# A transformer layer on one core: attention steps in one fixed form, with maxima on row tiles, projections at step ends, and row scaling on ScalarE

## What is computed

```
x = x + layernorm(attention(layernorm(x)))
x = x + layernorm(ffn(layernorm(x)))

attention: kqv = x @ Wqkv + bqkv            (16 heads of 32)
  scores = k . q / sqrt(32), kept where t >= s, else -10000
  attn = softmax(scores, axis=2); out = attn^T v; out @ Wo + bo
ffn: h = silu(x @ Wg^T) * (x @ Wu^T), h @ Wd^T
  with weights (int - 128) * scale, 2048 hidden
```

## Time and profile before

| | |
|---|---|
| median of 3 runs | 1860.55 us |
| the profiled execution | 1863.75 us |
| its span, first to last instruction | 1862.0 us |
| mean granted TensorE clock | 0.971 |
| busy: PE, DVE, ACT, POOL | 1719.7, 1062.0, 716.1, 332.4 us |
| chain that ended last, by engine | PE 72%, DVE 16%, ACT 3%, issue 3%, DMA 2% |
| first score of group 0 | at 114.92 us |
| first matmul of the feed-forward part | at 1156.63 us |

### The profile page before, as it was taken

How to read it: one execution, slowest core, us unless ns; L and a number is a source line. 1 busy time by engine, 2 the same in 40 slices (tenths; PEclk the granted TensorE clock), 3 DMA queues, 4 the chain that set the end, 5 groups by cost and what they waited for, 6 DMA issues and landing times.

```text
span 1862.0 us, 25259 instructions
## 1 busy us (share of the span) xinstructions
PE 1719.7 (92%) x10015; PEld 782.5 (42%) x10016; DVE 1062.0 (57%) x1779; ACT 716.1 (38%) x1271; POOL 332.4 (18%) x558
## 2 busy tenths in 40 slices
PE   3889899998899989899989788999999999999997
PEld 1433333343333333233333223555555555555554
DVE  5545864685864686765695576724343333434254
ACT  3335555444555445555435454222222222222221
POOL 2212222133222223222222133100000000000000
PEclk7989999999999999899999989999999999999999
DMA  5111111122111222101222255311010100101000
GB/s 175 35 35 36 37 44 35 47 74 86 51 31 35 59 70 78 51 19 35 69 68 69 58 189 161 120 35 45 23 46 29 40 35 34 40 30 39 29 23 23
DMA packets 59174, 104.17 MB, mean 56 GB/s; under 512 B 11440, under 2 KB 11440, under 8 KB 59056
## 3 DMA queue, kind: packets, MB, share of 16 engines
q1 hardware_dynamic: 59056, 102.56, 18.3%
HBM read 51.92 MB, written 25.17 MB: 41 GB/s over the span
## 4 chain that ended last, share of the span: by engine, by line
PE 72%; DVE 16%; ACT 3%; issue 3%; DMA 2%; SPq 2%; POOL 1%; DVEq 0%; ACTq 0%; POOLq 0%
PE ps L669 24%; PE ps L686 13%; PE ps L578 8%; PE ps L634 6%; PE ps L644 6%; DVE mcol L872 5%; PE ps L601 4%; PE ps L620 4%; PE ps L589 4%; DVE st L779 2%; PE ps L655 2%; SPq L469 2%; DVE rec L900 2%; ACT pt L748 1%; PE ps L559 1%
## 5 line engine op out<-in xcount | busy, mean ns | idle before, releaser
L748 ACT ACTIVATE pt<-ps,nrm 128x512 f32<-128x512 f32 (+3 forms) x768 | 389.5, 584 | 363.7 <-PE ps L620 363.4
L669 PE MATMUL ps<-x2in,gu 128*128 128x512 f16 x2048 | 463.9, 380 | 0.0
L872 DVE TENSOR_REDUCE mcol<-ps 128x1 f32<-128x512 f32 (+3 forms) x608 | 357.4, 650 | 141.0 <-PE ps L604 128.4
L669 PEld LDWEIGHTS ps<-x2in,gu 128*128 128x128 f16 x2048 | 190.8, 98 | 244.4 <-issue 31.6
L601 PE MATMUL ps<-kpack,qpack 96*128 96x512 f16 (+3 forms) x768 | 218.3, 333 | 47.9 <-DVE yt L910 17.9
L944 DVE SCALAR_TENSOR_TENSOR hf<-ps,usc,sg 128x512 f32<-128x512 f32 x128 | 96.2, 751 | 270.0 <-PE ps L669 268.7
L686 PE MATMUL ps<-wd,hh 128*128 128x512 f32 x512 | 224.0, 438 | 0.0
L620 PE MATMUL ps<-qpack,kpack 98*128 98x512 f16 (+3 forms) x768 | 201.3, 335 | 18.5 <-DMA qpack<-mt 8.2
L686 PE MATMUL ps<-wd,hl 128*128 128x512 f32 x512 | 200.7, 392 | 0.0
L994 POOL TENSOR_SCALAR rs<-mv 128x1 f32<-128x1 f32 x128 | 26.3, 205 | 921.5 <-DVE mv L781 921.5
L634 PE MATMUL ps<-pt,v 128*32 128x512 f32 (+3 forms) x1536 | 172.4, 522 | 17.4 <-DVE atf L896 14.8
(11 more groups left out here) (103 smaller groups left out, 1622.8 us busy)
## 6 DMA issues: line engine op xcount, KB each, us to landing
qpack<-stage SPq DMA_DIRECT2D x192, 64.0 KB, 2.0
kpack<-stage SPq DMA_DIRECT2D x192, 64.0 KB, 2.0
xin<-in_x SPq DMA_DIRECT2D x32, 256.0 KB, 2.6
xr<-in_x SPq DMA_DIRECT2D x32, 256.0 KB, 2.9
x1d<-x SPq DMA_DIRECT2D x32, 256.0 KB, 3.2
x2d<-x2s SPq DMA_DIRECT2D x32, 256.0 KB, 2.0
x2in<-x2d SPq DMA_DIRECT2D x8, 1024.0 KB, 5.6
x1in<-x1d SPq DMA_DIRECT2D x8, 1024.0 KB, 5.7
```

The source lines that it names most:

```text
L669: mm = pe.matmul(bk, GU[:, c, m, i * 128:(i + 1) * 128], x2in[:, 1 - k, :, p, c, :], start=p == 0 and c == 0, stop=p == 1 and c == 3)
L748: act.activation(Pt[:, (step - 1) % 2, h, off:512], ps[:, BANK[job], off:512], ACT.Exp, scale=esc).then_inc(s_ex, 1)
L872: dve.tensor_reduce(mcol[:, n % 2, col:col + step * (nh - 1) + 1:step], ps[:, BANK[job], 0:nh * w].rearrange("p (h k) -> p h k", h=nh), AX ...
```

## The change

- **Steps of one form.** Each step is now: one lot of maxima, den and num of the step before, four scores, what closes a half, row work, at most one projection at its end. Den and num thus stand ahead of the scores of the step, where they stood behind them. `projections` puts one projection at the end of the steps of width 512 and 384 (with gaps where there are fewer), none at the narrow ones. woproj are spread over the last group of their sequence and the first two of the next; `atT` has a fifth slot for that.
- **Row-tiled maxima.** A lot is now one block of queries for four heads: four matmuls with K = 32 on four row tiles (`tile_position`), each into its own bank, from `stage`, the projection's result, and not from the packed tiles. 12 lots per group, 48 reduces of one head each. The widths follow the width of the step.
- **Banks.** Maxima, scores and transposes take five banks in turn; projections have the sixth for themselves.
- **Row work.** `row_work` places it by the room of each step. ln1_norm, norm2 and the scaling of the attention output (wo_z) are now done by ACT with a scale and a bias from POOL (`dev`, three small operations in place of two).
- **Ends of halves.** The pull is gone. DVE transposes den in blocks of 32, takes the reciprocal of 128x16, transposes back, and multiplies num in one operation out of PSUM.
- In the last two groups the weights of the feed-forward part are spread over 20 steps. Three woproj stand in group 15, and five in the feed-forward part (four in each before).

```diff
-LOTS = max_lots()
+LOTS = [(2, 0, 384), (1, 0, 256), (0, 0, 128), (3, 0, 512), (6, 512, 384), (5, 512, 256), (4, 512, 128),
+        (4, 0, 512), (5, 0, 512), (6, 0, 512), (7, 0, 512), (7, 512, 512)]
+
+
+LN1 = ("ln1_stats", "ln1_norm", "ln1_turn")
+LN2 = ("wo_stats", "wo_z", "residual", "norm2", "turn2")
+DEV_FOR = {"ln1_norm": "ln1_stats", "wo_z": "wo_stats", "norm2": "residual"}
...
+def projections(n):
+
+    b, g = divmod(n, 4)
+    out = {}
+    if n + 2 < NG:
+        for i, s in enumerate(((1, 5, 7, 9), (0, 1, 4, 5), (1, 5, 7, 9), (1, 5, 6, 8))[g]):
+            out[s] = ("qk", n + 2, i % 2, i // 2)
+    if n == 0:
+        for i, s in enumerate((0, 4, 6, 8)):
+            out[s] = ("vproj", 4 + i)
+    if b + 1 < B:
+        first = 8 * b + 8 + (0, 0, 2, 6)[g]
+        for i, s in enumerate(((), (7, 9), (0, 4, 6, 8), (0, 4))[g]):
+            out[s] = ("vproj", first + i)
+    if g == 3:
+        for i, s in enumerate((5, 7, 9) if n == NG - 1 else (7, 9)):
+            out[s] = ("woproj", 8 * b + i)
+    elif b > 0 and g < 2:
+        for i, s in enumerate(((0, 4, 6, 8), (6, 8))[g]):
+            out[s] = ("woproj", 8 * b - 8 + (2, 6)[g] + i)
+    return out
...
+        for s, (j, kb) in enumerate(STEPS):
+            room[12 * n + s] = (33, 32, 8, 6)[max(0, kb - 4 * j)] - (24 if s in (0, 4) else 10 if s == 9 else 0)
+        for s, job in projections(n).items():
+            if job[0] != "qk":
+                room[12 * n + s] -= 7
+    cost = {"ln1_stats": 9, "ln1_turn": 7, "wo_stats": 9, "residual": 17, "turn2": 7}
...
-                    plan.extend(lot)
+            lot, of = (s + 3, n + 1) if s < 9 else (s - 9, n + 2)
+            if of < NG:
+                add(("mjob", of, lot))
             if pend is not None:
+                plan += [("den",) + pend, ("num",) + pend]
+            plan += [("score", n, j, kb, h) for h in range(4)]
+            if pend is not None and pend[2] == 4 * pend[1] + 3:
+                plan += [("invert",) + pend[:2], ("normalise",) + pend[:2]]
+            if s == 9 and n + 1 < NG:
+                plan += [("mjoin", n + 1), ("mturn", n + 1)]
+            here = rows.get(12 * n + s, [])
+            plan += [job for job in here if job[0] in ("ln1_turn", "turn2")]
+            for job in here:
+                if job[0] not in ("ln1_turn", "turn2"):
+                    plan += with_dev(job)
+            if n >= NG - 2:
+                plan += [("ffn_load", i) for i in range(24) if ffn_step(i) == 12 * (n - NG + 2) + s]
+            if s in ends:
+                add(ends[s])
             pend = (n, j, kb)
...
+        uses = [("max",) + job[1:] + (h,) for h in range(4)]
+    elif kind in ("qk", "vproj", "woproj") and attention and not feed:
+        take(job, 5)
+        continue
...
+        take(use, turn % (4 if feed else 5 if attention else 6))
...
-        atT = [A(f"at{p}", [128, 4, S], F16) for p in "hl"]
+        atT = [A(f"at{p}", [128, 5, S], F16) for p in "hl"]
...
+                    stage = stages[n % 2]
+                    qb, k0, w = LOTS[i]
+                    diag = k0 + w == (qb + 1) * 128
+                    e.wait_ge(s_qh, NO["qk", n, 0, qb // 4])
+                    e.wait_ge(s_qh, NO["qk", n, 1, (k0 + w - 1) // 512])
+                    for h in range(4):
+                        bk = bank(("max", n, i, h))
+                        rows = slice(32 * h, 32 * h + 32)
+                        mm = pe.matmul(bk[:, 0:w], stage[rows, 0, 0, qb * 128:(qb + 1) * 128],
+                                       stage[rows, 1, 0, k0:k0 + w], start=True, stop=not diag,
+                                       tile_position=(32 * h, 0))
+                        if not diag:
+                            mm.then_inc(s_mx, 1)
...
-                        e.wait_ge(s_nm, 2 * n + j)
+                        e.wait_ge(s_at, 2 * n + j)
...
-                        e.wait_ge(s_rc, 2 * n + j)
+                        e.wait_ge(s_dt, 2 * n + j)
+                    if kb >= 4 * j:
+                        e.wait_ge(s_dg, 8 * n + 4 * j + kb - 4 * j + 1)
...
+            def normalised(dst, src, job):
+
+                m = (STAT[job] - 1) % 6
+                e.wait_ge(s_nb, NO[("dev",) + job])
+                return act.activation(dst, src, ACT.Identity, scale=rs[:, m, 1:2], bias=rs[:, m, 2:3])
...
+                elif kind in ("ln1_norm", "norm2"):
+                    t = a[0]
+                    no = NORMED["ln1_turn" if kind == "ln1_norm" else "turn2", t]
+                    if no > 2:
+                        e.wait_ge(s_tr, TURN_OF[no - 2])
+                    src, of_stats = (xin, "ln1_stats") if kind == "ln1_norm" else (x1, "residual")
+                    normalised(xn[:, (no - 1) % 2, :], src[:, t % 2, :], (of_stats, t)).then_inc(s_xn, 1)
+                elif kind == "wo_z":
+                    t = a[0]
+                    if t >= 2:
+                        e.wait_ge(s_xn, NORMED["turn2", t - 2])
+                        e.wait_ge(d_o1[t % 2], 16 * (t // 2))
+                    normalised(x1[:, t % 2, :], yt[:, t % 2, :], ("wo_stats", t)).then_inc(s_z, 1)
...
                     if step > 2:
-                        e.wait_ge(s_den, step - 2)
+                        e.wait_ge(s_num, step - 2)
...
+                    for h in range(4):
+                        col = h * 8 + qb if k0 == 0 else 32 + h * 4 + qb - 4
+                        e.wait_ge(s_mx, reduced(n, i, h))
+                        dve.tensor_reduce(mcol[:, n % 2, col:col + 1], ps[:, BANK["max", n, i, h], 0:w], AX.X, ALU.max
+                                          ).then_inc(s_mr, 1)
...
-                elif kind == "pull":
+                elif kind == "invert":
+                    n, j = a
+                    e.wait_ge(s_den, STEP[n, j, 4 * j + 3])
+                    dve.transpose(rec[:], DEN).then_inc(s_dt, 1)
+                    e.wait_ge(s_dt, NO[job])
+                    dve.reciprocal(inv[:], rec[:, 0:512:32]).then_inc(s_iv, 1)
+                    e.wait_ge(s_iv, NO[job])
+                    dve.transpose(rec[:], inv[:].unsqueeze(2).to_broadcast([128, 16, 32])).then_inc(s_rc, 1)
+                elif kind == "normalise":
                     n, j = a
                     if NO[job] > 1:
                         e.wait_ge(s_al, NO[job] - 1)
-                    e.wait_ge(s_den, STEP[n, j, 4 * j + 3])
-                    dve.tensor_scalar(atf[:], NUM, beta, None, ALU.mult).then_inc(s_nm, 1)
-                elif kind == "invert":
-                    n, j, c = a
-                    e.wait_ge(s_rc, NO["pull", n, j])
-                    dve.reciprocal(rec[:, c * 128:c * 128 + 128], rec[:, c * 128:c * 128 + 128]).then_inc(s_iv, 1)
-                elif kind == "normalise":
-                    n, j = a
-                    e.wait_ge(s_nm, NO[job])
-                    e.wait_ge(s_iv, 4 * NO[job])
-                    dve.tensor_tensor(atf[:], atf[:], rec[:], ALU.mult).then_inc(s_at, 1)
+                    e.wait_ge(s_rc, NO[job])
+                    e.wait_ge(s_num, STEP[n, j, 4 * j + 3])
+                    dve.scalar_tensor_tensor(out=atf[:], in0=NUM, scalar=beta, in1=rec[:], op0=ALU.mult, op1=ALU.mult
+                                             ).then_inc(s_at, 1)
                 elif kind == "woproj":
+                    t = a[0]
                     e.wait_ge(s_small, SCALED)
                     e.wait_ge(d_rows, 64)
+                    if t >= 2:
+                        e.wait_ge(s_z, NO["wo_z", t - 2])
                     e.wait_ge(s_wo, NO[job])
```

More of the change, by code:

```diff
@@ L60, in order_of_jobs @@
     add = plan.append
-    ln1 = ("ln1_stats", "ln1_norm", "ln1_turn")
-    wo = ("woproj", "residual", "norm2", "turn2")
-    first = staged(ln1, list(range(8)))
+    first = [[each for job in lot for each in with_dev(job)] for lot in staged(LN1, list(range(8)))]
     add(("load_x", 0))
@@ L87, in order_of_jobs @@
     for i in range(len(LOTS)):
         add(("mjob", 0, i))
[L89 removed]
+        if fill and i % 3 != 2:
             add(fill.pop(0))
[L91 to L100 removed]
@@ L102, in weigh @@
-    def weigh(step, between):
-        n, j, kb = step
-        add(("num",) + step)
-        for lot in between:
-            plan.extend(lot)
-        add(("den",) + step)
-        if kb == 4 * j + 3:
-            add(("pull", n, j))
-            late.extend([("invert", n, j, c) for c in range(4)] + [("normalise", n, j)])
+    plan += [("mjoin", 0), ("mturn", 0), ("packs", 1)] + [("mjob", 1, i) for i in range(3)] + [("ffn_scales",)]
+    rows = {}
+    for job, step in row_work().items():
+        rows.setdefault(step, []).append(job)
@@ L155, in order_of_jobs @@
         if n + 2 < NG:
             add(("packs", n + 2))
-    weigh(pend, [])
-    plan += late
+    plan += [("den",) + pend, ("num",) + pend, ("invert",) + pend[:2], ("normalise",) + pend[:2]]
+    tail = [with_dev(job) for s in range(12) for job in rows.get(12 * NG + s, [])]
```

(29 more changed lines are left out.)

334 lines of the change are left out of this document (150 added, 184 removed).

## The result

The kernel after the change takes **1890.0 us** (median of 4 runs, 1888.4 to 1890.4), the kernel before on the same chip 1862.3 us (4 runs, 1857.3 to 1865.2). The ratio is 1.015, 95% interval 1.0126 to 1.0175: slower by 1.5%, where 1817 us and a gain were forecast. It lies above the range, too. The profiled execution has a span of 1886.6 us for 1862.0, and a mean granted clock of 0.944 for 0.971.

What follows compares the result with a forecast made beforehand. PE, or what PE waits for, bounds the kernel. Attention: 946 + 26 - 14 + 15 + 20 = 993 us for 1041.7; with 2.6 behind and about 2 ahead, 44 less, so 1817 us, range 1778 to 1862.

Steps and rivals of the forecast that it cites:

- The three scalings moved to ACT cost nothing there.: Attention: the fullest wide step gives ACT 5.8 us, about a step, hidden by PE; cost nothing.
- The clock term: Narrow steps of the attention: PE idles, the clock halves; 12 falls, 20 us, with ends none and 32 (54 us).
- Rival 3: Narrow steps: the clock falls at every narrow pair, 20 more stretches, 34 us, giving 1851 us; chance 0.12.
- DVE's lateness: Attention steps: DVE waits for ACT's copy, so reduces hold scores; 5.5 us per sequence, 15 in all.
- step table: Attention, one group: step times by width, from 2.83 to 6.07 us, sum 59.1 us; sixteen groups 946.
- Rival 4: Attention: DVE late twice as often, waits growing into each other, 15 to 25 us, giving 1837 us; chance 0.13.
- Ahead of the first scores: Before the attention: group 0's reduces cost about 2 us more.
- Behind the attention: Feed-forward part: it gets one woproj more, 2.6 us.
- rival 1: Maxima: row tiles run one behind the other, 58 us, giving 1875 us, slower than before; chance 0.06.
- rival 2: Tiling switches: full drains, 0.17 us for 0.10, 31 us in all, giving 1848 us; chance 0.09.
- the first group of a sequence: Attention: this group would be no longer than the others, with groups of 59 to 64 us throughout.
- the transposes: Attention: 0.71 us each, 49 in all, 13 in steps that wait anyway; 26 us added.

Runs made afterwards that it cites:

- experiment 1: The changed kernel with POOL's three small operations (dev) issued right behind the statistics they belong to: 1848.2 us, ratio 0.9918 to the kernel before.
- experiment 8: The changed kernel with POOL's operations right behind their statistics and all three scalings back on DVE: 1849.2 us, ratio 0.9917 to the kernel before.
- the fill: The changed kernel with four unread 512-column matmuls at the end of each narrow step (256 and 128 wide): 1854.3 us, ratio 0.9946 to before.
- experiment 5: The changed kernel with POOL's operations right behind their statistics and four unread matmuls in each narrow step: 1815.0 us, ratio 0.9741 to before.

## Why the prediction was wrong

The forecast for the attention was 993 us, measured were 1049.5; 984 with both causes mended.

- **The failed step: "The three scalings moved to ACT cost nothing there."** It counted ACT's time in a wide step and did not ask when the scale and the bias are there. `dev` stood in the account of the change as "three small operations in place of two", but the change also moved them. Before, POOL did its part within the job of the statistics (`ln1_stats`, `woproj`, `residual`); `with_dev` puts it in the step of the scaling, and experiment 1 puts it back. POOL's queue was never walked: the step's triangle is ahead of `dev`, and the exponentials of the next step are behind the scaling. The bullet costed a full wide step, while the statistics of the first tiles hit the narrow ones, where ACT has no slack. Cost: 42 us (experiment 1), of which 32 in the profiled attention and 2.8 ahead of it; some 10 of the 32 are the 39 us fewer at half clock, at 0.25. The scaling itself does cost nothing on ACT, as the bullet says (experiment 8). Late statistics with the scaling on DVE were not run, so what the late place alone would have cost stays open. None of the rivals had it.
- **The clock term was too small by its amount.** Forecast: 12 falls of 3.4 us, 20 us. Measured: 24 stretches with 176 us, at 0.25 us per us 44 us. Most of them last 6.8 to 10.2 us, where the sum had 3.4 for each, from one fall read before. Rival 3 had the mechanism and its sign ("more than 20 stretches at half clock") and priced it at 34 us on top; the fill gave 36. Rival 3 alone would still have been faster than before; only with the late statistics beside it does the time leave the range.
- **DVE's lateness, "5.5 us per sequence, 15 in all": right.** The waits list hides it, the starts of the scores show it: in group 4, step 6, 1.03 us where the sum had 1.5, over the attention 15 us in the kernel after and 20 in experiment 5, there 5.8 in groups 4 to 7. DVE's wait for ACT's copy is there, too (63.0 us). 0.34 us of it in the first step of most groups (6.36 us for 6.02) is nearly all by which quiet groups exceed the step table. Rival 4, twice the lateness, is out.
- **Ahead of the first scores "about 2 more": 11.2.** 3 to 6 of them went with early statistics (120.2 to 123.4 us); of the 5.7 that experiment 5 still lacks, 2.8 are the later end of group 0's maxima, near the 2 of the sum, and 2.9 the four lots that now stand ahead of the first scores, which were in the code and not in the sum. Behind the attention 2.6 was forecast and 5.6 came, 2.9 in experiment 5.
- **What held.** The step table (59.1, measured 59.5), row tiles side by side (rival 1 is out), 0.10 us for their switch (rival 2 is out; the drain that the Trainium skill, "TensorEngine Tiling", Key Properties, describes showed no more than this tenth), the first group of a sequence down from 87.4 us, and the transposes. With its two faults mended the kernel takes 1815.0 us for a forecast of 1817; that this is so near is partly luck: the term for falls was 13 us too high (27 us at half clock in experiment 5, at 0.25 us each 7 for 20), lateness 5 and the start 4 us too low.
- **Where the expected gain of the row tiles went** is the surprise: not off the critical path, but to the clock (table above).

## What to carry to other kernels

When work moves to another engine, walk the queue of the engine that feeds it as well as its own: a helper of 1.2 us behind the wrong instruction held ScalarE for 93 us here, and putting it directly behind its input was worth 2%. Take a saving on TensorE at its full value only if TensorE is not left idle more by it; here 32 us of saved maxima came back as half clock until some throw-away matmuls stood in the gaps. When the list of waits is short, look at the starts of single matmuls before you call a wait absent. And sum up a step table per group without side work first: the groups that match it tell at once that the miss is in the side work.
